# A graph network's edge sort: preset pieces between its steps, table round trips at its end, and its steps in another order of work

## The reference

```
edge_index = stack([src, dst])
h = relu(layernorm(x)); x = x + L0(h, edge_attr_16, edge_index, ...)   # 3 message layers, sum over dst
h = relu(layernorm(x)); x = x + L1(h, edge_index, edge_attr_32, ...)   # gated messages, sum over src
h = relu(layernorm(x)); x = x + L2(h, edge_index)                      # sum of x[src] over dst
h = relu(layernorm(x)); x = x + L3(h, edge_index, edge_attr_32, ...)   # linear messages, sum over dst
return x
```

## Time and profile before

| | us |
|---|---|
| median of 3 runs (11978.92 to 11989.2) | 11985.75 |
| the profiled execution | 11980.92 |
| its span in the trace | 11979.2 |
| stage 1, counting, in the trace | 0 to 183.26 |
| sort stage, from its first DMA to POOL's last scatter's issue | 183.26 to 2292 |

### The profile page before, as it was taken

One profiled execution on the slowest core, in us unless ns is written; L12 is line 12 of the kernel. 1 busy time (PEld: TensorE's weight loads), 2 busy tenths in 40 slices (PEclk: granted clock), 3 DMA queues, 4 the chain that ended last, 5 costly groups with the idle time before them and its releaser, 6 DMA issues. The chain is left out here.

```text
span 11979.2 us, 359391 instructions
## 1 busy us (share of the span) xinstructions
PE 7965.9 (66%) x118914; PEld 6443.5 (54%) x118915; DVE 6872.1 (57%) x17994; ACT 5925.7 (49%) x15268; POOL 6924.6 (58%) x7153
## 2 busy tenths in 40 slices
PE   4666666555678887788877788767777544435556
PEld 3444444344566666666666666666555433433554
DVE  5766666544358885266652566644888862135331
ACT  0444444455259995288862678733777541014000
POOL 0777777766038884088860788711888704630761
PEclk9999999855899998999989999989999897669775
DMA  8111111499986665955549555669777598779983
GB/s 354 60 41 41 41 42 41 140 382 382 276 295 196 197 196 161 382 164 164 164 113 386 195 162 163 129 282 372 225 226 226 169 374 282 226 218 402 300 291 84
DMA packets 1254072, 2559.22 MB, mean 214 GB/s; under 512 B 293083, under 2 KB 632300, under 8 KB 1231086
## 3 DMA queue, kind: packets, MB, share of 16 engines
q1 hardware_dynamic: 913742, 1398.19, 35.2%
q0 software_dynamic: 232416, 575.55, 16.5%
q10 hardware_dynamic: 107712, 582.79, 11.8%
HBM read 1590.32 MB, written 965.35 MB: 213 GB/s over the span
## 5 line engine op out<-in xcount | busy, mean ns | idle before, releaser
L624 POOL DMA_INDIRECT by_src<-sort_rec,slots x1560 | 1527.4, 979 | 748.9 <-issue 747.1
L1233 POOL DMA_INDIRECT NEAR<-spread_f,gather_ids_l x1368 | 1393.0, 1018 | 452.2 <-issue 207.5
L1334 ACT ACTIVATE zr_l<-z_l,stat_l 128x64 f32<-128x64 f32 x5472 | 1372.1, 336 | 0.1
L744 PE MATMUL bank<-hots_t 104*128 104x128 bf16 (+3 forms) x1568 | 610.3, 464 | 471.6 <-ACT junk L610 471.6
L1363 PE MATMUL bank<-NEARB,hot_t_l 128*128 x16416 | 783.3, 198 | 132.6 <-issue 54.1
L1363 PEld LDWEIGHTS bank<-NEARB,hot_t_l 128*128 128x128 bf16 x16416 | 664.1, 100 | 317.2 <-issue 268.7
L1395 PE MATMUL bank<-m_l,NEAR 128*128 128x64 bf16 x5472 | 570.7, 194 | 372.2 <-issue 261.5
L1375 PE MATMUL bank<-wm_diag,zr_t_l 128*128 128x128 f32 x5472 | 803.4, 291 | 0.9 <-issue 0.9
L1242 POOL TENSOR_TENSOR rest_l<-m_l 128x512 f32<-128x512 f32 x684 | 717.5, 1049 | 70.5 <-DVE m_l L1297 58.9
L1375 PEld LDWEIGHTS bank<-wm_diag,zr_t_l 128*128 128x128 f32 x5472 | 671.9, 193 | 160.4 <-issue 160.4
L1223 POOL TENSOR_TENSOR piece_l<-rest_l 128x512 bf16<-128x512 f32 x684 | 710.8, 1039 | 59.9 <-POOL rest_l L1242 12.4
(11 more groups left out here) (374 smaller groups left out, 25736.4 us busy)
## 6 DMA issues: line engine op xcount, KB each, us to landing
unit_hot_a<-src_hots_t SPq DMA_DIRECT2D x342, 512.0 KB, 5.0
spread_f<-unit_rows_a ACTq DMA_DIRECT2D x342, 512.0 KB, 6.7
hot_t_l<-dst_hots_t SPq DMA_DIRECT2D x456, 256.0 KB
NEAR<-dst_hots SPq DMA_DIRECT2D x456, 256.0 KB, 2.8
spread<-sum_unit_rows ACTq DMA_DIRECT2D x114, 768.0 KB, 8.9
spread<-last_unit_rows ACTq DMA_DIRECT2D x114, 768.0 KB, 9.0
src_hots<-move_hot SPq DMA_DIRECT2D x114, 512.0 KB
src_hots_t<-move_hot_t SPq DMA_DIRECT2D x114, 512.0 KB
```

Source lines behind the costliest of these rows:

```text
L624: pool.indirect_dma_start(out=by_src, out_offset=bass.IndirectOffsetOnAxis(ap=slots[h][:, j:j + 1], axis=0), in_=rec[h][:, j, :], in_offse ...
L744: pe.matmul(to, lhsT=cols[:, t * P:width], rhs=cols[:, 0:width], start=True, stop=False, skip_group_check=True)
L1233: pool.indirect_dma_start(out=far_in[h % WA][:, g * GT:(g + 1) * GT, :].rearrange("p j f -> p (j f)"), out_offset=None, in_=spread_f, in_o ...
L1334: last = act.activation(zr[h % 2][:, t, :], z[h % 2][:, t, :], ACT.Relu, scale=stat[h % WA][:, 2, t:t + 1])
```

## The change

- Preset pieces have 38 rows instead of 57, 48 pieces instead of 32, for both orders.
- The preset of `by_dst` is no longer issued ahead of the sort's first tick. ACT issues one piece at the start of every fourth tick, from octet 4 to octet 192.
- The two round trips of the group tables move from the end of stage 1 to the end of SP's work in the sort stage, and the two orders' trips overlap.
- There are four one-hot buffers, four `hots_t`, four `rank`, eight `tables` and two `place` instead of 2, 2, 2, 2 and 1. Stage 1 clears and fills the larger sets.
- The sort's ticks are in another order, with lags up to 4 on ACT and DVE and up to 3 on PE. Growth is computed ahead of the look-up. DVE ranks one comparison per half (256 wide), ACT three (512, 384 and 128 wide). The slots of an octet are settled once, not per half.

```diff
-FILL = 57
+FILL = 38
...
-        hots = [ob(f"hots{k}", [P, 2 * OC, WB], BF16) for k in range(2)]
+        hots = [ob(f"hots{k}", [P, 2 * OC, WB], BF16) for k in range(4)]
...
-        tables = [ob(f"tables{k}", [WB, 2, 2, NW], FP16) for k in range(2)]
+        place = [ob(f"place{k}", [WB, NW]) for k in range(2)]
+        tables = [ob(f"tables{k}", [WB, 2, 2, NW], FP16) for k in range(8)]
...
-                for o in range(2):
-                    sp.wait_ge(win4_ready, 2 * (o + 1))
...
-                    sp.wait_ge(windows_out[o], 64)
...
+                for t in place + tables:
+                    then(dve, dve.memset(t[:], 0.0))
...
+                    sp.wait_ge(win4_ready, 4)
+                    for o in range(2):
+                        sp.dma_start(window_row[o].rearrange("a (p c) -> (a p) c", p=P),
+                                     win4_i[:, 1 - o, :]).then_inc(windows_out[o], 16)
...
-                    for k in range(NS // P // FILL):
-                        act.dma_start(by_dst[0:NS, :].rearrange("(p r) f -> p r f", p=P)[:, k * FILL:(k + 1) * FILL, :],
-                                      fill[:]).then_inc(filled_dst, 16)
...
+                    def ranks(h, n, u):
+
+                        m = 2 * (n - 1) + u + 1
+                        act.wait_ge(s["compared_s"], m)
+                        at_least(act, s["slot"], n - WS)
+                        for k, t in enumerate((3, 2, 0)):
+                            act.activation(junk[t][:], compared(u, t), ACT.Relu, bias=minus_one[:],
+                                           accum_out=rank[h][:, 4 * u + t:4 * u + t + 1]).then_inc(s["ranked_s"], 1)
...
                     def tick(part):
                         if p := part(0):
                             h, st, n, nth = p
+                            if h == 0 and not (isinstance(nth, int) and not 2 <= nth <= NS // P // FILL + 1):
+                                fill_dst(nth - 2)
+                        if p := part(2):
+                            h, st, n, nth = p
                             act.wait_ge(s["hots_turned"], n)
-                            at_least(act, s["looked"], 2 * (n - 2))
...
+                        if p := part(4):
+                            h, st, n, nth = p
+                            ranks(h, n, 1)
+                        if p := part(3):
...
+                        if p := part(3):
+                            h, st, n, nth = p
+                            ranks(h, n, 0)
...
+                    def tick(part):
+                        if p := part(4):
+                            h, st, n, nth = p
+                            pick(h, n, 1)
+                        if p := part(2):
+                            h, st, n, nth = p
+                            grow(h, n, 1)
+                        if p := part(4):
+                            h, st, n, nth = p
+                            rank_middle(h, n, 0)
+                            rank_middle(h, n, 1)
...
+                            window_hots(dve, hots[h], st * OC).then_inc(s["hots_ready"], 1)
+                        if p := part(3):
+                            h, st, n, nth = p
+                            pick(h, n, 0)
                         if p := part(1):
                             h, st, n, nth = p
...
+                            grow(h, n, 0)
+                        if p := part(4):
+                            h, st, n, nth = p
+                            settle(h, n, nth)
...
+                        if p := part(1):
+                            h, st, n, nth = p
+                            grow(h, n, 0)
+                        if p := part(3):
+                            h, st, n, nth = p
+                            look(h, n, 0)
+                        if p := part(3):
+                            h, st, n, nth = p
+                            at_least(pe, s["ranked_s"], 6 * (n - 2) + 3)
+                            for t in (3, 2, 0):
+                                last = compare(h, 0, t)
+                            last.then_inc(s["compared_s"], 1)
...
+                            at_least(pe, s["ranked_s"], 6 * (n - 1))
+                            for t in (3, 2, 0):
+                                last = compare(h, 1, t)
+                            last.then_inc(s["compared_s"], 1)
+                        if p := part(1):
+                            h, st, n, nth = p
+                            grow(h, n, 1)
+                        if p := part(3):
+                            h, st, n, nth = p
+                            look(h, n, 1)
```

More of the change, by code:

```diff
@@ L552, in sort_edges, with compared @@
             steps = NOCT
-            def compared(t):
-                bank, at, width = blocks[t]
-                return same[bank][:, at:at + width]
+            def compared(u, t):
+                if t == 1:
+                    return middle[:, 2 * P * u:2 * P * (u + 1)]
+                bank, at = {3: (wide, 0), 2: (mixed, 0), 0: (mixed, 3 * P)}[t]
+                return bank[u][:, at:at + (t + 1) * P]
             with nc.Block() as block:
@@ L716, in _, with grow @@
-                    rolling(dve, steps, WS, 1, tick)
+                            grow(h, n, 0)
+                        if p := part(4):
+                            h, st, n, nth = p
+                            settle(h, n, nth)
+                    rolling(dve, steps, WS, 4, tick)
                 @block.tensor
                 def _(pe):
-                    def tick(part):
-                        if p := part(0):
+                    def grow(h, n, u):
+                        m = 2 * (n - 1) + u + 1
+                        pe.wait_ge(s["hots_ready"], n)
+                        at_least(pe, s["moved"], 3 * (m - 2))
+                        at_least(pe, s["picked"], m - 6)
+                        for c in range(4):
+                            last = pe.matmul(grown[u], lhsT=hots[h][:, 2 * (4 * u + c), 0:NW],
+                                             rhs=hots[h][:, 2 * (4 * u + c) + 1, 0:NW], start=c == 0, stop=c == 3)
+                        last.then_inc(s["grown"], 1)
@@ new lines, in look @@
+                    def look(h, n, u):
+                        m = 2 * (n - 1) + u + 1
+                        pe.wait_ge(s["turned_sb"], n)
+                        at_least(pe, s["moved"], 3 * (min(m + 2, 2 * steps) if isinstance(m, int) else m + 2))
+                        at_least(pe, s["picked"], m - 2)
+                        for c in range(4):
+                            for q in range(2):
+                                last = pe.matmul(looked[u][:, c * 2 * NW:(c + 1) * 2 * NW],
+                                                 lhsT=hots_t[h][0:WB, (4 * u + c) * P:(4 * u + c + 1) * P],
+                                                 rhs=tables[2 * h + u][:, q, :, :].rearrange("p o w -> p (o w)"),
+                                                 start=q == 0, stop=q == 1, skip_group_check=True)
+                        last.then_inc(s["looked"], 1)
```

215 lines of the change are left out of this document (90 added, 125 removed).

## The result

The changed kernel takes **11883.78 us** (median of 4 runs, 11880.05 to 11887.67) where the kernel before takes 11984.19 us (4 runs, 11978.92 to 11989.2). The ratio is 0.9916, its 95% interval 0.9899 to 0.9933. The profiled execution took 11887.67 us, its span is 11885.7 us; it stands to before's 11980.92 and 11979.2 us.

The account below looks back on a forecast made before the run. POOL's scatters were taken to pace the sort at 10.28 us per octet, so its start counts. 12.5 + 90.0 - 3.9 - 2.5 = 96.1 us off 11985.75 gave a forecast of 11890 us, range 11866 to 11930.

Parts of the forecast that it names:

- round trips out of stage 1: End of stage 1: without SP's trips the sort begins at 170.8 instead of 183.26, -12.5 us.
- seven more clears: Stage 1: clearing ten tiles instead of three takes 2.1 us more, hidden while DVE idles for the keys; nothing.
- preset out of ACT's way: Sort's begin: ACT comes to its table load at once instead of 89.96 us later, -90.0 us.
- first octet's way: Sort's begin: a longer chain through the engines puts POOL's first scatter 16.9 us in instead of 12.97, +3.9 us.
- 48 pieces under the sort: Sort stage: preset pieces beside POOL's scatters lengthen some of them, +2.5 us, bounds 0 to 19 us.
- order of work: Sort stage: other engines' order, lags and buffers stay off the path at 10.28 us per octet; nothing.
- trips at the end: End of the sort: SP's trips, near 2130, finish ahead of the last scatter; nothing, 16 us at most if exposed.
- second rival: Sort: DVE's wider reductions hold POOL's scatters, 108 us lost, 11998 us; chance 2%.
- first rival: Sort: a ring between PE and ACT, put at 7.0 us per octet, is slower than POOL's 10.28; up to 12227 us; chance 4%.
- Pieces hurt each time: Sort: each preset piece lengthens one scatter by 0.40 us, or two; 11906 to 11930 us; chance 8%.
- the change doesn't do what it says: Stage 1 or first tick held by something else, only the 90 us or part come; 11902 or 11912 us; chance 5%.
- The last step: Stages behind the sort: only shifted, as long as before, so the whole 96.1 us comes off the total.

Follow-up runs that it names:

- e3: Kernel before with only the group tables' round trips moved to the end of SP's work in the sort: 11960.26 us, ratio 0.9987.
- e4: Changed kernel with the one-hots' column numbers in PSUM instead of SBUF, and PE's second growth count waiting for the one-hots: 11849.54 us, ratio 0.9894.
- e1: Changed kernel with the 48 preset pieces of `by_dst` issued ahead of the sort again: 11976.45 us, ratio 1.0002.
- e6: Changed kernel with POOL sending only 2 of the 8 scatters of each octet: 11293.16 us, one run.
- e9: Kernel before, old order, with preset pieces between octets, trips at the sort's end and the one-hots' column numbers in PSUM: 11844.56 us, ratio 0.9891.

## Why the prediction was right, and where it was not

The predicted 11890 us stands against 11883.78. By the prediction's own steps:

| step | predicted | measured |
|---|---|---|
| round trips out of stage 1 | sort begins at 170.8, -12.5 us | 170.38, -12.9 (e3: -13.7) |
| seven more clears | 0 | 0 |
| preset out of ACT's way | -90.0 | ACT's table load at 170.38 instead of 273.22; of these 102.8 us, 12.9 are the trips' |
| first octet's way | +3.9, first scatter at 187.7 | +3.4, at 186.70 |
| 48 pieces under the sort | +2.5 (0 to 19) | some 2 at most where no lock is taken (e4); scatters +14 in all |
| order of work | 0 | not by waiting; part of the 14, by way of the lock |
| trips at the end | hidden, near 2130 | hidden, 2137 to 2144 |
| sum at the sort's end | -96.1 | -85.4 |
| stages behind | as long as before | 8 us shorter |

**The start** came out within a microsecond in each of its terms. ACT's copy came 2.6 us behind its table load, as put down, and the first scatter 16.3 us behind the sort's begin where the chain of hand-offs had given 16.9. e1 shows from the other side how much of the gain is this move's: with the preset in front the ratio is 1.0002, though 12.4 us of that are the longer queue of 48 pieces.

The **clears** had one surprise. In DVE's row, a small cast of 4 numbers:

```profile
4.49 6.10 DVE L364 CAST small<-group_ids 128x4 f32<-128x4 int32 x1
...
9.51 0.85 POOL L286 MEMSET stage<- 128x896 f32 x1
...
10.36 0.19 POOL L289 MEMSET ones_b<- 3x128 bf16 x1
...
10.82 0.98 DVE L368 TENSOR_SCALAR windows<-keys_i 128x1568 int32<-128x1568 int32 x1
```

It stands for 6.10 us and ends at 10.59, just behind POOL's row of clears (10.55); before, this cast took 0.18 us. Before, two other casts took 2.60 and 2.52 us instead of 0.30 and 0.33 beside POOL's clear of `fill`, and DVE's step of 2.38 us overlapped another clear. This looks like the same lock with POOL as its holder; no run tried it. It cost nothing: the 2.38 us step now takes 0.98 us and ends at 11.80 instead of 12.34.

**What failed is the size of what slows scatters in the sort**: the sum had 2.5 us for the pieces and nothing for the order of work, 14 us were measured, and the missing term is the lock beside L232. The number was inside the bounds of the pieces' term, but for the wrong reason. The bound of 0.40 us per piece came from a long scatter of 1.37 us that I put down to the draining preset, and the scatters of 1.31 and 1.33 us I called POOL's loop pass. They come once per pass, but they are all scatters that start inside L232. The 2.5 us came from early scatters of 1.14 us; the very first one takes that in every kernel, with or without a preset in flight, and the one at 294.01 starts inside an L232 too. DVE's rows beside them, which I didn't lay next to POOL's, would have shown it before any run. The second rival belongs here: I asked whether the reduction of the earlier trace rows locks POOL out and wrote that the trace has no sign of a lock in this stage. It had one in 39 scatters, 13.4 us between 400 and 2000 us, only beside another instruction. The reductions, and the DVE steps with a PSUM operand, leave scatters alone. The rival's mechanism was true, its instruction and its price (108 us) were not.

**The first rival**, the ring, was priced at 7.0 us per octet and runs in 6.35 (e6); giving it little chance was right. "Pieces hurt each time" and "the change doesn't do what it says" did not happen.

**The last step** was only half right. Behind the sort the spans are 9682.1 us before (11979.2 - 2297.12) and 9674.0 after (11885.7 - 2211.73); in e3, whose later stages are those of before too, 9676.9, in e9 9665.0. These stages vary by up to 17 us from kernel to kernel with nothing changed in them. The 11 us that the sum had too much at the sort's end and the 8 us that came from behind it nearly cancel; the total is closer than its terms, and that is luck. The spread of the runs adds to it: the two spans differ by 93.5 us, the two medians by 100.4. What moves those stages was not tried.

## What to carry to other kernels

When a long queue of transfers goes out from an engine that must start the next stage, look for a later place in small pieces: here 48 pieces of 1064 KB ahead of the octets cost 102 us, and between them 2 us at most by themselves, though the sort became 6.5 to 12 us longer with them because DVE and POOL met more often. Before you call an odd duration a loop's or a transfer's, lay the other engines' rows beside it, above all DVE's beside indirect DMAs from POOL; here a DVE instruction with two SBUF operands that was running when such a DMA started was paid on POOL up to its end, less 0.13 us, and one operand in PSUM took the cost away although DVE's own time went from 0.59 to 1.02 us. Speeding up engines that aren't the bound brought nothing (8.35 to 6.35 us per octet under a bound of 10.28), but it did shift who meets whom.

## What the runs showed of the hardware

- An indirect DMA on POOL that starts while DVE runs the one-hots (bf16, two SBUF inputs, 0.59 us) is longer by DVE's end - its start - 0.13 us, to 0.01 us in 116 scatters of one trace; if the DMA starts before or up to 0.044 us behind the DVE instruction, it keeps its 0.97 us, and the DVE instruction takes up to 0.67 us (e1).
- The same comparison with its column numbers in PSUM takes 1.02 us and lengthens none of the 134 scatters that start inside it (e4, 400 to 2000 us); the whole sort is then 1988.67 to 1989.25 us for 1563 scatters.
- A reduction on DVE (128x784 f32 in SBUF, one input) lengthened none of the 193 scatters that started well inside it in after by more than 0.013 us.
- Moving 51 MB (48 x 1064 KB) from ACT's queue beside POOL's scatters added some 2 us at most to their sum where no lock was taken (e4), with the DMA engines' share up from 0.16 to 0.21 or 0.22 in after.
- 48 transfers of 1064 KB issued in a row hold ACT 102.33 us, 32 of 1596 KB with the same bytes 89.93 us.
